# A recurrent block with a gated feed-forward: a third place for the products of input and B, one transposed input, and a new order laid on the same engines

## The reference

```python
xn = layernorm(x)                                  # x: 4 x 4096 x 512
# branch 1, on every second token (2048 of 4096)
xs = xn[:, ::2]; xs = xs * rsqrt(mean(xs**2) + 1e-6) * g_norm
x_proj, gate = split(xs @ w_in.T + b_in)           # 512 + 512
h = tanh(h * A + x_proj[t][:, :, None] * Bm)       # 2048 steps; h: 4 x 512 x 64
y = h @ Cm.sum(0) + Dv * x_proj[t]
s = repeat((y * silu(gate)) @ w_out.T + b_out, 2)
# branch 2, on every token
spikes = sigmoid(xn @ W_enc + b_enc)               # 512 -> 1024
cont = spikes @ W_s2c + b_s2c                      # 1024 -> 64
gate8 = two best of softmax(cont @ Wr + br), weights summing to 1
e = sum_e gate8[e] * (relu(cont @ W1[e] + b1[e]) @ W2[e] + b2[e])   # 8 experts, 64 -> 512 -> 64
decoded = sigmoid(e @ W_c2s + b_c2s) @ W_dec + b_dec                # 64 -> 1024 -> 512
out = x + s * silu(layernorm(decoded) * ln_g + ln_b)
```

## Time and profile before

| | |
|---|---|
| median of 3 runs | 5803.54 us (5798.73 to 5804.52) |
| the profiled execution | 5802.78 us |
| its span, first to last instruction | 5801.0 us |
| granted TensorE clock, mean of the span | 0.996 |
| TensorE busy (matmuls) | 5580.6 us, 96% |
| TensorE weight loads | 3073.1 us, 53% |
| VectorE | 5403.5 us, 93% |
| GpSimd | 5287.9 us, 91% |
| ScalarE | 4595.4 us, 79% |
| DMA | 673.41 MB, mean 116 GB/s |

### The profile page before, as it was taken

The page is one execution under the profiler, slowest core; times in us unless marked ns, Lnnn a source line. Parts: engine busy times, 40 slices in busy tenths (PEclk is TensorE's granted clock), DMA queues, the critical chain, the costliest instruction groups (busy, mean ns, idle before and its releaser), DMA issues.

```text
span 5801.0 us, 88242 instructions
## 1 busy us (share of the span) xinstructions
PE 5580.6 (96%) x28770; PEld 3073.1 (53%) x28770; DVE 5403.5 (93%) x9108; ACT 4595.4 (79%) x9941; POOL 5287.9 (91%) x2828
## 2 busy tenths in 40 slices
PE   6999999999999999999999999999999999999998
PEld 3555555555555555555555555555555555555554
DVE  5999999999999999999999999999999999999997
ACT  5878878788788787887887878878878788788786
POOL 5999999999999999999999999999999999999997
PEclk9999999999999999999999999999999999999999
DMA  6454544544444445444454454444444444444443
GB/s 166 113 121 107 122 115 111 123 112 116 120 108 121 116 111 122 112 116 120 108 120 117 110 121 113 115 120 109 119 118 110 120 114 114 120 110 118 119 109 88
DMA packets 158222, 673.41 MB, mean 116 GB/s; under 512 B 45761, under 2 KB 46785, under 8 KB 92225
## 3 DMA queue, kind: packets, MB, share of 16 engines
q1 hardware_dynamic: 157762, 667.76, 48.0%
HBM read 617.26 MB, written 50.33 MB: 115 GB/s over the span
## 4 chain that ended last, share of the span: by engine, by line
PE 76%; ACT 14%; DVE 7%; issue 3%; SPq 1%; DMA 0%; POOL 0%; ACTq 0%; POOLq 0%
PE bank L973 17%; PE bank L921 15%; PE ps_y L887 11%; PE ps_acc L985 9%; PE bank L1037 8%; PE ps_acc L1037 8%; ACT h L598 4%; PE bank L908 4%; DVE ps_z L1144 4%; ACT conte L707 3%; DVE ps_z L1138 2%; ACT wide L718 1%; PE bank L1020 1%; PE ps_acc L1020 1%; PE bank L959 1%
## 5 line engine op out<-in xcount | busy, mean ns | idle before, releaser
L525 POOL TENSOR_TENSOR u<-xb,bt 128x1024 f32<-128x1024 f32 x2048 | 4811.0, 2360 | 387.1 <-DVE ps_z L1144 315.6
L598 ACT ACTIVATE h<-ps_z 128x512 f32<-128x512 f32 x4096 | 2408.0, 599 | 1008.3 <-DVE ps_z L1144 807.9
L1138 DVE TENSOR_TENSOR ps_z<-h,ps_A 128x512 f32<-128x512 f32 x4096 | 2664.7, 691 | 314.7 <-ACT h L598 233.1
L1144 DVE TENSOR_TENSOR ps_z<-ps_z,u 128x512 f32<-128x512 f32 x4096 | 2655.3, 691 | 0.0
L973 PE MATMUL bank<-wide,w 65*128 65x256 f32 x4096 | 1015.0, 393 | 18.5 <-ACT wide L718 18.5
L887 PE MATMUL ps_y<-h,c_wide 128*32 128x512 f32 x8192 | 962.0, 599 | 49.0 <-ACT h L598 49.0
L921 PE MATMUL bank<-xnT,w_enc 128*128 128x256 f32 x4096 | 901.3, 381 | 2.8 <-ACT wide L671 2.8
L973 PEld LDWEIGHTS bank<-wide,w 65*128 65x128 f32 x4096 | 730.6, 189 | 315.3 <-issue 152.6
L921 PEld LDWEIGHTS bank<-xnT,w_enc 128*128 128x128 f32 x4096 | 772.9, 190 | 158.9 <-issue 53.3
L887 PEld LDWEIGHTS ps_y<-h,c_wide 128*32 128x32 f32 x8192 | 227.2, 109 | 566.8 <-issue 418.1
L908 PE MATMUL bank<-w_in,xnT 128*128 128x512 f32 x1024 | 474.4, 606 | 7.6 <-DVE c_wide L1214 1.6
(11 more groups left out here) (124 smaller groups left out, 4285.1 us busy)
## 6 DMA issues: line engine op xcount, KB each, us to landing
xb<-x_proj_scratch SPq DMA_DIRECT2D x2048, 256.0 KB, 4.6
xbuf<-in_L_attn_x SPq DMA_DIRECT2D x256, 128.0 KB
xres<-in_L_attn_x SPq DMA_DIRECT2D x512, 64.0 KB
out<-g SPq DMA_DIRECT2D x256, 128.0 KB
x_proj_scratch<-xp SPq DMA_DIRECT2D x256, 64.0 KB
w_in<-in_L_attn_w_in SPq DMA_DIRECT2D x1, 2048.0 KB, 8.1
w_enc<-in_L_ffn_W_enc SPq DMA_DIRECT2D x1, 2048.0 KB, 16.5
w_dec<-in_L_ffn_W_dec SPq DMA_DIRECT2D x1, 2048.0 KB, 20.4
```

Source lines behind the costliest of these rows:

```text
L525: pool.tensor_tensor(u[:, tau % 2, :, :], xt, bt[:, :, :], ALU.mult).then_inc(u_ready, 1)
L598: act.activation(h[:, tau % RING, f, :], ps_z[:, f, :], ACT.Tanh).then_inc(h_ready, 1)
L1138: dve.tensor_tensor(ps_z[:, f, :], h[:, (tau - 1) % RING, f, :], ps_A[:, f, :], ALU.mult).then_inc(m_done, 1)
L1144: dve.tensor_tensor(ps_z[:, f, :], ps_z[:, f, :], u[:, tau % 2, f, :], ALU.add).then_inc(z_ready, 1)
```

## The change

1. `u` gets three places (`URING = 3`), indexed by the step's number over the whole run; GpSimd waits for the addition three steps back.
2. `xnT` has one place instead of one for even and one for odd blocks.
3. All slots are laid anew, for the kernel with 1 and 2; the queue of SyncE stays.
4. Of the shaping ahead of the first block, the centring of w_dec (8 instructions on ScalarE, one a step in steps 7 to 14) and the decoder's bias (4 on VectorE, in steps 3 to 6) move into the first block; the second input product of block 0 moves ahead of the column sums, which are now taken of the unshaped w_s2c and w_dec.

The slots that the prediction speaks of, and the code that changed. Slots that are left out moved within the same group of their engine or by less than a step, save the slots of TensorE, whose other numbers changed with the sequence kept. The three readers and writers of `xnT` that only lose the index `par` are left out too.

```diff
+URING = 3
-POOL_PROJ_SCALE = -23.875
-POOL_DEC_SCALE = (31.8125, 34.6875)
-POOL_FIN_SKIP = 0.4375
-POOL_FIN_GATE = 36.3125
-POOL_FIN_ADD = (43.375, 59.1875)
-ACT_PROJ_OUT = (-20.4375, -7.25)
-ACT_FIN_Y = 33.8125
-ACT_CONTT_COPY = 6.8125
-ACT_RELU = (13.375, 13.875, 14.5625, 14.75, 15.5, 15.5625, 16.5625, 16.5625, 17.8125, 17.8125, 18.8125, 20.9375, 21.625, 21.875, 22.6875, 22.8125)
-ACT_DEC_SILU = (31.5, 39.9375)
-ACT_PROJ_SUM = (-29.25, -29.0625)
-ACT_PROJ_VAR = -25.0625
-ACT_OUT_SEED = 38.9375
-ACT_DEC_SEED = (26.3125, 27.875)
-PE_Y = (19.1875, 20.375, 21.5, 34.8125, 34.9375, 37.25, 38.125, 38.375)
-PE_PROJ_TRANSPOSE = (-12.0, -10.625)
-PE_ROUTER = 19.0625
-PE_GATET = 21.4375
-PE_FIN_TRANSPOSE = 50.8125
-DVE_ROUTE = (7.75, 8.75, 9.375, 9.5, 9.625, 9.75)
-DVE_DEC_SCALE = (31.625, 35.8125)
-DVE_DEC_SHIFT = (31.8125, 37.9375)
+POOL_PROJ_SCALE = -22.375
+POOL_DEC_SCALE = (32.75, 35.5625)
+POOL_FIN_SKIP = 5.625
+POOL_FIN_GATE = 37.875
+POOL_FIN_ADD = (43.25, 60.25)
+ACT_SHAPE = (7.5, 8.5, 9.5, 10.5, 11.5, 12.5, 13.5, 14.5)
+ACT_PROJ_OUT = (-20.125, -7.4375)
+ACT_FIN_Y = 35.6875
+ACT_CONTT_COPY = 6.875
+ACT_RELU = (13.1875, 13.9375, 13.9375, 14.75, 15.5625, 15.625, 16.8125, 16.875, 17.5625, 17.875, 18.6875, 19.6875, 21.5625, 21.5625, 22.5, 22.5625)
+ACT_DEC_SILU = (32.5625, 38.8125)
+ACT_PROJ_SUM = (-30.0625, -29.375)
+ACT_PROJ_VAR = -24.125
+ACT_OUT_SEED = 38.6875
+ACT_DEC_SEED = (26.125, 28.875)
+PE_Y = (20.4375, 25.0625, 28.25, 36.6875, 36.9375, 40.75, 45.625, 46.3125)
+PE_PROJ_TRANSPOSE = (-9.125, -4.75)
+PE_ROUTER = 22.5625
+PE_GATET = 27.0625
+PE_FIN_TRANSPOSE = 52.3125
+DVE_SHAPE = (3.0, 4.0, 5.0, 6.0)
+DVE_ROUTE = (8.6875, 9.0, 9.3125, 9.6875, 9.6875, 9.75)
+DVE_DEC_SCALE = (31.8125, 35.75)
+DVE_DEC_SHIFT = (32.0625, 37.875)
...
         h = sb("h", [P, RING, F, D])
         xb = sb("xb", [P, 2, CK, D])
-        u = sb("u", [P, 2, F, D])
+        u = sb("u", [P, URING, F, D])
         xbuf = sb("xbuf", [P, 2, D])
         xres = sb("xres", [P, D])
-        xnT = sb("xnT", [P, 2, KD, 2, P])
+        xnT = sb("xnT", [P, KD, 2, P])
         xp = sb("xp", [P, 2, D])
...
                 if tau % CK == 0:
                     pool.wait_ge(chunk_loaded[c % 2], 16 * B * (4 * blk + c // 2 + 1))
-                if not (is_first(blk) and tau < 2):
-                    pool.wait_ge(z_ready, 2 * STEPS * blk + 2 * tau - 2)
+                t = STEPS * blk + tau
+                if t >= URING:
+                    pool.wait_ge(z_ready, 2 * (t - URING) + 2)
                 xt = xb[:, c % 2, tau % CK, :].unsqueeze(1).to_broadcast([P, F, D])
-                pool.tensor_tensor(u[:, tau % 2, :, :], xt, bt[:, :, :], ALU.mult).then_inc(u_ready, 1)
+                pool.tensor_tensor(u[:, t % URING, :, :], xt, bt[:, :, :], ALU.mult).then_inc(u_ready, 1)
             def proj_scale(blk):
...
                 at = (blk, FILL_ENC + k)
                 wait_filled(act, at)
+                if k == 0 and not is_first(blk):
+                    wait_dec_filled(act, blk - 1, 1)
                 drained(half_tanhs(bank[k % 2], k, b_enc_col), at)
...
                 else:
                     act.wait_ge(acc_drained, 2 * blk + 1)
+                if is_first(blk):
+                    act.wait_ge(biases_steps, 4)
                 act.activation(dec_out[q][:, :], b_dec_all[:, :], ACT.Copy).then_inc(dec_seeded, 1)
             def acc_seed(blk):
-                if not is_first(blk):
+                if is_first(blk):
+                    act.wait_ge(biases_steps, 1)
+                else:
                     wait_dec_drained(act, blk - 1, 1)
...
             proj_seed(0, 1)
             proj_out(0, 0, 0)
+            proj_out(0, 0, 1)
             act.wait_ge(early_loaded, EARLY)
-            act.wait_ge(leads_made, 1)
+            act.activation(b_enc_col[:, :], b_enc_col[:, :], ACT.Copy, scale=0.5)
+            act.activation(b_c2s_col[:, :], b_c2s_col[:, :], ACT.Copy, scale=0.5)
+            act.activation(ln_g_all[:, :], ln_g_all[:, :], ACT.Copy, scale=D ** 0.5)
+            act.wait_ge(columns_summed, 1)
+            act.activation(cont_bias[0:M, :], ps_y[0:M, 0:1], ACT.Identity, scale=0.5, bias=cont_bias[0:M, :]
+                           ).then_inc(biases_shifted, 1)
+            act.activation(w_s2c[:, :, :], w_s2c[:, :, :], ACT.Copy, scale=0.5)
+            act.wait_ge(leads_made, 3)
             for half in range(2):
                 rows = slice(M * half, M * half + M)
                 act.activation(w_r[rows, E * E:E * E + M], ident[rows, rows], ACT.Copy)
-            act.wait_ge(weights_shaped, 1)
-            act.activation(w_dec_shift[:, :], w_dec_sum[:, :], ACT.Copy, scale=-0.5 / D).then_inc(weights_shaped, 1)
-            act.activation(w_s2c[:, :, :], w_s2c[:, :, :], ACT.Copy, scale=0.5)
-            act.activation(b_enc_col[:, :], b_enc_col[:, :], ACT.Copy, scale=0.5)
-            act.activation(b_c2s_col[:, :], b_c2s_col[:, :], ACT.Copy, scale=0.5)
-            act.activation(ln_g_all[:, :], ln_g_all[:, :], ACT.Copy, scale=D ** 0.5)
-            act.wait_ge(weights_shaped, 2)
-            for k in range(KH):
-                ins = act.activation(w_dec[:, k, :], w_dec[:, k, :], ACT.Identity, bias=w_dec_shift[:, k:k + 1], scale=0.5)
-            ins.then_inc(weights_shaped, 1)
-            act.wait_ge(columns_summed, 1)
-            act.activation(cont_bias[0:M, :], ps_y[0:M, 0:1], ACT.Identity, bias=cont_bias[0:M, :]).then_inc(biases_shifted, 1)
-            act.wait_ge(biases_shifted, 2)
+            act.wait_ge(biases_shifted, 1)
             act.activation(acc_row[0:M, 0:T2], acc_row[0:M, 0:T2], ACT.Identity, bias=cont_bias[0:M, :]).then_inc(acc_shaped, 1)
             act.wait_ge(acc_shaped, 1)
-            proj_out(0, 0, 1)
+
+            def shape_decoder(k):
+
+                if k == 0:
+                    act.wait_ge(weights_shaped, 1)
+                    act.activation(w_dec_shift[:, :], w_dec_sum[:, :], ACT.Copy, scale=-0.5 / D).then_inc(weights_shaped, 1)
+                    act.wait_ge(weights_shaped, 2)
+                    act.wait_ge(columns_summed, 2)
+                ins = act.activation(w_dec[:, k, :], w_dec[:, k, :], ACT.Identity, bias=w_dec_shift[:, k:k + 1], scale=0.5)
+                if k == KH - 1:
+                    ins.then_inc(decoder_shaped, 1)
             def between(blk, par, slot):
+                for k in range(KH):
+                    if slot == ACT_SHAPE[k]:
+                        if is_first(blk):
+                            shape_decoder(k)
                 if slot == ACT_PROJ_NORM:
...
                             ins.then_inc(acc_filled, 1)
             def decode(blk, q):
+                if is_first(blk) and q == 0:
+                    pe.wait_ge(decoder_shaped, 1)
                 pe.wait_ge(dec_seeded, 2 * blk + q + 1)
...
             pe.wait_ge(ready, 2)
             proj_in(0, 0, 0)
-            pe.wait_ge(weights_shaped, 3)
+            proj_in(0, 0, 1)
+            pe.wait_ge(early_loaded, EARLY)
             zeros = h[:, RING - 1, 0, :]
             pe.matmul(ps_y[:, :], zeros[:, 0:P], zeros, start=True, stop=True)
             for k in range(KH):
-                pe.matmul(ps_y[0:M, 0:1], w_s2c[:, k, :], ones[:, 0:1], start=False, stop=(k == KH - 1),
-                          skip_group_check=True)
+                ins = pe.matmul(ps_y[0:M, 0:1], w_s2c[:, k, :], ones[:, 0:1], start=False, stop=(k == KH - 1),
+                                skip_group_check=True)
+            ins.then_inc(columns_summed, 1)
             for k in range(KH):
...
                 for half in range(2):
                     if slot == PE_PROJ_IN[half]:
-                        proj_in(blk, par, half)
+                        if not is_first(blk):
+                            proj_in(blk, par, half)
                 for n in range(4):
...
                         dve.wait_ge(u_ready, STEPS * blk + tau + 1)
                     dve.wait_ge(m_done, t2 + f + 1)
-                    dve.tensor_tensor(ps_z[:, f, :], ps_z[:, f, :], u[:, tau % 2, f, :],
+                    dve.tensor_tensor(ps_z[:, f, :], ps_z[:, f, :], u[:, (STEPS * blk + tau) % URING, f, :],
                                       ALU.add).then_inc(z_ready, 1)
...
             ins.then_inc(ready, 1)
             dve.wait_ge(early_loaded, EARLY)
-            dve.tensor_reduce(w_dec_sum[:, :], w_dec[:, :, :], AX.X, ALU.add).then_inc(weights_shaped, 1)
             given = w_r[:, E * E:E * E + E]
...
                 dve.tensor_tensor(acc_row[:, c0:c0 + E * E].rearrange("p (e j) -> p e j", e=E),
                                   br_all[:, :].unsqueeze(1).to_broadcast([P, E, E]),
-                                  br_all[:, :].unsqueeze(2).to_broadcast([P, E, E]), ALU.subtract)
-            dve.tensor_reduce(b_dec_sum[:, :], b_dec_all[:, :], AX.X, ALU.add).then_inc(biases_steps, 1)
-            dve.wait_ge(biases_steps, 1)
```

(28 more changed lines are left out.)

63 lines of the change are left out of this document (32 added, 31 removed).

## The result

| | before | after |
|---|---|---|
| median (runs) | 5804.52 us (5798.73 to 5820.89, 11) | 5827.29 us (5814.12 to 5841.25, 11) |
| the profiled execution, its span | 5802.78, 5801.0 | 5817.06, 5815.3 |
| granted TensorE clock, mean of the span | 0.996 | 0.995 |
| TensorE, VectorE, GpSimd, ScalarE busy | 5580.6, 5403.5, 5287.9, 4595.4 | 5581.9, 5406.0, 5290.1, 4589.4 |

The ratio is 1.0032 (95% interval 1.0023 to 1.0041): slower by about 0.3%, where 5814 (+0.18%) was forecast. Two groups stand in the 11 runs after: four at 5814.1 to 5817.1 with a mean clock of 0.995 to 0.996, seven at 5826.2 to 5841.3 with 0.991 to 0.994. The profiled execution is of the lower group, 14.28 us above the profiled one before. These 14.28 us are explained first; the groups, to which the rest of the 22.8 us between the medians belongs, have a part of their own further down.

The account below looks back on a forecast made before the run. Bound: TensorE's own work plus a 16.64 us leg through ScalarE and VectorE per block. 5802.8 + 4.1 (first block) + 6.3 (steady blocks) = 5813.2; with the median 0.76 above the profiled run, 5814, range 5795 to 5830.

Parts of the forecast that it names:

- u and xnT: Third place for u and single xnT: each worth 0, since VectorE never waits for u and xnT adds no wait.
- GpSimd's wait would be hardly smaller: Steady blocks: GpSimd's waiting for VectorE, 315.6 us in all before, was to stay nearly as large.
- +0.10 a block: Steady blocks: later routing lengthens the leg through ScalarE and VectorE by 0.10, 63 times, +6.3 us.
- Item 2: Step 8: routing's first operation between the additions costs 0.27 instead of 0.11, the reduction nothing; +0.19 at step 9's additions.
- item 3: At the gate: xnT's evacuation, which held things back by 0.09, no longer waits for TensorE; +0.10 remains.
- the stall at the projection sum: First block: ScalarE stands from about 53 to 71.6 awaiting the next input; of 15.8 us ahead, 2.3 remain.
- the shapings: First block: eight w_dec shapings in steps 7 to 14 cost 3.05 by the first expert matmul, 0.4 more at relu 1.
- 4.1: First block's total loss in us: 0.65 at step 7, plus 3.05 and 0.4; bounds -2.7 and +8.
- the bias terms: First block, steps 3 to 6: unhidden bias shaping of 0.66, 0.6, 0.1 and 0.6, about 1.2 net.
- my 1.75: First block: encoder group 2 at TensorE's lower clock after idling makes the spikes wait 1.4 to 2.1, taken as 1.75.
- the second rival: Steady blocks: later logits or ScalarE's fuller groups miss their slot, 0.3 to 0.5 a block, 5824 to 5836; chance 0.20.
- the stated range: Whole kernel: 5795 to 5830 us, leaving out the faster rival and part of the slower one.

Follow-up runs that it names:

- e1_ring: Kernel before with three places for u and single xnT, old order and shaping kept: 5803.36 us, ratio 0.999.
- e2_order: Kernel before with three places for u, single xnT and the new slot order, all shaping still ahead of the first block: 5811.88 us, ratio 1.0006.
- e6_route: Changed kernel with routing's first operation behind both additions of step 8 (slot 8.75 instead of 8.6875): 5817.65 us, ratio 1.0025.
- e9_routes: Changed kernel with the first y group back behind the router and old slots for routing, its tanh and gate: 5863.93 us, ratio 1.0096.
- e5_hold: Changed kernel with chunk 2 in the first block issued only once the input of block 1 has landed: 5814.87 us, ratio 1.0016.
- e11_warm: Changed kernel with the encoder's second fill done six times in the first block to keep TensorE busy: 5830.90 us, ratio 1.0046.
- e3_first: Kernel before, old order, two places for u, single xnT, with the shaping moved into the first block: 5821.69 us, ratio 1.0016.
- e10_again: Changed kernel timed once more without any edit: 5827.23 us, ratio 1.0038.
- e4_xearly: Changed kernel with chunk 1 and the input of block 1 issued ahead of the late weights: 5810.76 us, ratio 1.0005.
- e7_shape: Changed kernel with w_dec's shapings in steps 16 to 23 and the last three of the bias in 20 to 22: 5816.53 us, ratio 1.0012.
- e12_spread: e8_join with the loads cut up and issued in the order the first block needs them: 5790.26 us, ratio 0.9979.
- e8_join: Kernel before's steady order with early start, late shapings, three places for u, and chunk 1, input and Dv loaded ahead: 5802.26 us, ratio 0.9997.

## Why the prediction was nearly right, and where it fell short

**u and xnT: right.** e1_ring: no change. That GpSimd's wait would be hardly smaller was wrong (315.6 to 122.9 in e1_ring, to 210.4 in the changed kernel), and it made no difference, as the prediction's own argument said.

**Steady blocks: right in size, partly by luck.** +0.10 a block was forecast, 0.07 to 0.08 measured: 6.3 against 4.6 us. e2_order puts it on the order alone. Item 2 laid it on the place of routing's first operation between the two additions of step 8 and gave nothing to the reduction ("VectorE would have waited for the second tanh there"); e6_route refutes the first and its rows the second: there ScalarE was through with step 8 at 3041.16 (tanh from 3039.96, 1.20 long), the reduction holds the second multiplication from 3041.29 to 3041.48, and 0.17 are found at `sel`, against the +0.19 of item 2. So the size was met by another operation. The 0.10 that come back before the gate are close to item 3's 0.09. In the changed kernel itself the first operation delays the second addition of step 8, and the multiplication behind the reduction needs that addition's tanh, so its rows don't part the two. e9_routes shows that routing can't go back by itself; which of ScalarE's shifts forced it later was not taken apart further.

**First block: the way right, one term too small.** The start (50.3 measured, 50.2 forecast), the stall at the projection sum and the shapings' 3.75 (3.05 and some 0.7 of bias) came as forecast. From the landing to the first expert matmul my walk gave 105.87 + 3.7 - 71.6 = 37.97; five profiled runs (the changed kernel twice, e5_hold, e6_route, e11_warm) have 37.2 to 37.8. What failed is the sentence "Chunk 1 lands 7.5 to 9.4 us after issue, about 68.7; DMA traffic ends early in the window from 71.5, at about 71.6: that is the input". The landing was read from a trace in which nothing followed the input for 10 us. It came at 76.8, 5.2 later, and 4.1 + 5.2 = 9.3 is the measured 9.4, outside the bounds that I had set for the first block (-2.7 to +8). I had the mechanism as a bound of 2 us ("input 2 us later because chunk 2 is now issued right behind it"). e5_hold measures it at 4.0 (landing at 72.86), and e3_first, with nothing behind the input either, agrees with at most 10.8 us from issue to the end of the traffic. The other 1.2 of the 5.2 stay open. Chunk 1 was late too (u(4) starts with it at 71.98, not 68.7), but the input came after it. Smaller: the bias terms of the prediction, 1.96 less the 0.5 that they replace, make 1.46 and not "about 1.2"; with that the 4.1 would have been 4.4.

**TensorE's clock: cheap in the profiled runs.** Encoder groups 2 and 3 took 10.22 in one run of the changed kernel and 8.97 in another (e10_again), and the first expert matmul came 37.84 and 37.47 after the landing: of 1.25 us, 0.37 went through. That is one pair of runs, but my 1.75 looks like an upper end.

**The sum.** 4.1 + 6.3 = 10.4 forecast, 9.4 + 4.6 = 14.0 found; the two misses have opposite signs. The lower group, 5814.1 to 5818.5 over both timings, is what was forecast.

**The median is not.** It lies in the upper group, at 5827, inside the time of the second rival (0.3 to 0.5 a block more; by the prediction's own terms some 5826 to 5839, not 5824 to 5836), whose mechanism is not there: the period is 89.24. So that the median fell into the stated range was luck. Over all timings the kernel before has 29 of 101 runs above 5810, the changed kernel 12 of 19 at 5825 or more, which is hardly chance (one-sided, 0.5%; this counts in the timing that raised the question; the second alone, five of eight against three of 20 beside it, gives 2%). Three profiles of kernels with the shaping in the first block (e3_first, e4_xearly, e9_routes) show a stretch of that block, between 110 and 150 us, in which TensorE is busy and granted the lower clock, some 12 us long in its effect; three profiles (e2_order, e4_xearly, e9_routes) show such a stretch in mid-run. No profile of the changed kernel itself fell in the upper group, so that its twelve runs there are of this kind is argued, not shown. Their mean clock fits: 0.993 to 0.994 at 5825 to 5831 against 0.995 to 0.996 below, where 25 us at half clock would lower the mean by 0.002 (an estimate from the spans). What in the start makes it likelier stays open: e7_shape, with the same stall, had none in 12 runs, e5_hold four in 12, e6_route five in 12, e12_spread, without the stall, three in 12.

## What to carry to other kernels

Work taken off the front of a kernel gives back only as much as the loads let it: find the load that is late next, and the next after that; here three stood in a row (the input, Dv, chunk 2), and laying them in the order of need took 12 us off (5802.26 to 5790.26). Don't read the landing of a transfer from a trace in which the queue behind it is empty if the edit fills it. And don't put back one engine's slots of an order that was laid for all: the y group that made routing late also covered a copy that had become later.

## What the hardware showed that I had not expected

A busy TensorE was granted the lower clock for some 20 us in mid-run (20.00 of 20.00 us busy at 0.50, 4590 to 4610 in e4_xearly), in a program that uses one core only, and runs that lie 12 to 15 us above the others are there with nearly every kernel here, the one before among them (29 of 101). And the issue of the loads moves by 4 us from run to run (the input at 57.2 in e6_route and at 61.2 in the changed kernel, by the same program up to there), which passes into the time where the kernel waits for its loads (encoder of block 1 at 164.08 and 169.00).

And the last operation of the bias, on VectorE with a single SBUF tensor, 0.48 us alone, took 2.11 beside a product on GpSimd (1.94 in e8_join and e12_spread, 1.35 in e10_again). In all nine profiles in which a product was under way it ends 0.27 to 0.29 us after the product. The Trainium skill, "SBUF — State Buffer", section "SBUF: two separate sides", says that the two engines share a pair of ports as an exclusive lock, held for a whole instruction, which for a VectorE operation with one SBUF input means one in a 2-port mode; the ends agree with the lock, and in which mode the operation ran no run here shows.
